# Linear attention with its first rows normed under the weight loads and its query squares on GpSimd; row attention with two groups of heads packed

## The reference

```python
def softmax_kernel_features(data, proj, is_query):          # 12 heads of 16, 44 features
    data_dash = jnp.einsum('bhnd,md->bhnm', data_normalizer * data, proj)
    diag_data = jnp.sum(jnp.square(data), axis=-1, keepdims=True) * 0.5 * data_normalizer ** 2
    stab = jnp.max(data_dash, axis=-1, keepdims=True) if is_query else jnp.max(data_dash)
    return ratio * (jnp.exp(data_dash - diag_data - stab) + EPS)
q, k, v = (x @ W_qkv)                                       # x is the layer-normed stream
q1, k1 = softmax_kernel_features(q, proj_mat, True), softmax_kernel_features(k, proj_mat, False)
kv, ksum = jnp.einsum('bhnm,bhnd->bhmd', k1, v), jnp.sum(k1, axis=2)
z = 1.0 / jnp.einsum('bhnm,bhm->bhn', q1, ksum)
out = (jnp.einsum('bhnm,bhmd->bhnd', q1, kv) * z[..., None]) @ W_proj + b_proj
...
attn = jax.nn.softmax(jnp.einsum('bhnd,bhmd->bhnm', q, k) * hd ** (-0.5), axis=-1)
o = jnp.einsum('bhnm,bhmd->bhnd', attn, v).transpose(0, 2, 1, 3).reshape(B, N, C)
return o @ proj_w + proj_b
```

## Time and profile before

| | us |
|---|---|
| three runs | 2276.53, 2280.19, 2281.41 |
| median | 2280.19 |
| profiled execution | 2284.59, span 2282.7 |
| TensorE busy in the span | 1844.9 (81%) |
| VectorE busy | 1344.2 (59%) |
| ScalarE busy | 1055.9 (46%) |
| GpSimd busy | 563.8 (25%) |
| linear attention, first block to its end | 109 to 490 |
| row attention, second block with its tail | 1632 to 1925 |

### The profile page before, as it was taken

One profiled execution on the slowest core, in us unless ns is written; L12 is line 12 of the kernel. 1 busy time (PEld: TensorE's weight loads), 2 busy tenths in 40 slices (PEclk: granted clock), 3 DMA queues, 4 the chain that ended last, 5 costly groups with the idle time before them and its releaser, 6 DMA issues. The chain is left out here.

```text
span 2282.7 us, 30822 instructions
## 1 busy us (share of the span) xinstructions
PE 1844.9 (81%) x9746; PEld 993.9 (44%) x9746; DVE 1344.2 (59%) x2464; ACT 1055.9 (46%) x1916; POOL 563.8 (25%) x708
## 2 busy tenths in 40 slices
PE   5789889958756447777489977999899993999998
PEld 4645755535324320000122244443134343888887
DVE  6446359946111779999678876999655553222211
ACT  2011322214001659999689964333387870222222
POOL 5000000000212017767200003332014443333333
PEclk9989999958887675555599978997699995999999
DMA  3010110024996005234101008788777634577774
GB/s 89 7 44 28 55 35 22 19 91 182 408 408 265 1 18 180 89 116 134 32 26 32 28 17 124 125 125 126 83 89 108 96 95 144 164 210 202 198 212 104
DMA packets 153120, 258.49 MB, mean 113 GB/s; under 512 B 28560, under 2 KB 124673, under 8 KB 148006
## 3 DMA queue, kind: packets, MB, share of 16 engines
q1 hardware_dynamic: 134822, 239.15, 39.8%
q0 software_dynamic: 18176, 17.80, 4.0%
HBM read 215.16 MB, written 57.51 MB: 119 GB/s over the span
## 5 line engine op out<-in xcount | busy, mean ns | idle before, releaser
L1734 PE MATMUL ps<-arena 128*128 x384 | 198.1, 621 | 82.8 <-ACT ps L1817 62.0
L1817 ACT ACTIVATE ps<-ps,arena 128x512 f32<-128x512 f32 x384 | 256.1, 724 | 9.1 <-POOL arena L1798 9.1
L1744 DVE TENSOR_REDUCE arena<-ps 128x1024 f32 x192 | 232.8, 1224 | 29.0 <-PE ps L1734 18.0
L2186 DVE TENSOR_REDUCE arena<-ps 128x1024 f32 x192 | 221.1, 1213 | 11.9 <-PE ps L2432 9.5
L2655 ACT ACTIVATE arena<-ps 128x1024 f32<-128x1024 f32 x192 | 185.8, 1022 | 90.6 <-PE ps L2533 89.5
L2992 ACT ACTIVATE arena<-ps,arena 128x256 f32<-128x256 f32 x234 | 89.7, 482 | 235.8 <-PE ps L2957 235.7
L2432 PE MATMUL ps<-arena 96*128 96x512 bf16 x500 | 163.6, 432 | 25.0 <-DVE arena L2186 11.5
L1976 ACT ACTIVATE arena<-ps 128x1024 f32<-128x1024 f32 x192 | 178.9, 1043 | 10.6 <-DVE arena L1996 5.2
L2927 POOL DMA_INDIRECT out_dram<-arena x78 | 121.2, 1554 | 238.6 <-DVE arena L3016 168.6
L3012 DVE TENSOR_TENSOR arena<-ps,arena 128x384 f32<-128x384 f32 x39 | 21.8, 558 | 258.7 <-PE ps L2968 258.7
L531 PE MATMUL ps<-arena 96*128 96x456 f32 (+1 forms) x512 | 168.7, 481 | 6.0 <-DMA arena<-la_xt 4.8
(11 more groups left out here) (395 smaller groups left out, 3144.9 us busy)
## 6 DMA issues: line engine op xcount, KB each, us to landing
arena<-in_sm_w_dram SPq DMA_DIRECT2D x128, 576.0 KB, 16.6
arena<-in_re_w_dram SPq DMA_DIRECT2D x39, 1252.0 KB, 5.9
arena<-ra_parts SPq DMA_DIRECT2D x192, 192.0 KB, 9.6
routed_in<-routed_in SPq DMA_DIRECT2D x8, 3332.0 KB, 14.0
ra_parts<-arena SPq DMA_DIRECT2D x48, 192.0 KB, 2.4
arena<-routed_in SPq DMA_DIRECT2D x39, 196.0 KB, 5.4
arena<-la_xt SPq DMA_DIRECT2D x16, 384.0 KB, 3.4
arena<-arena SPq DMA_DIRECT2D x64, 96.0 KB, 2.2
```

The lines of the kernel that those rows point to most:

```text
L1734: ins = pe.matmul(ps[:, 2 * (n % 4) + t % 2, :], QM[j][:, h, t * P:(t + 1) * P], KI[:, b, h // HG, :], start=True, stop=True)
L1744: v.tensor_reduce(MXq[:, b, 2 * u:2 * u + 2, at_head(h)], ps[:, 2 * (n % 4):2 * (n % 4) + 2, :], AX.X, ALU.max).then_inc(s_lk, 1)
L1817: ins = act.activation(bank, bank, ACT.Exp, bias=nb[n % 4][:, t % 2:t % 2 + 1], scale=c_reg, accum_out=RS[:, b, t, at_head(h):at_head(h) + 1])
L2186: v.tensor_reduce(MX[:, bass.ds(b, 1), 2 * (n % 2):2 * (n % 2) + 2, n // 2].rearrange("p o t -> p (o t)"), ps[:, 2 * (n % 2):2 * (n % 2) + ...
```

## The change

Three things. In the linear attention's first block the norm, the turn (into banks 4 and 5) and the copy of batch 0 now stand before the weight products and their results; the second half of the weight products (banks 4 to 7) waits for the copy; the 11 loads count on three semaphores, of which TensorE waits for `s_wt` (`WT` and `BD`), VectorE for `s_w` (`W`), and `s_wp` is awaited before the query block's products. In the query pass VectorE's product L820 is gone: GpSimd squares `SQ` in place when VectorE has copied it, and VectorE waits for it before the sum. In row attention the groups 0 and 1 are packed: `OP` takes group 0 to the first 16 of 32 columns and group 1 to the other 16, group 2 stands alone with zeros beside it, so that two transposes and a contraction over two groups are left; `OS` is one buffer; the rows of `Wp` come in 12 DMAs.

```diff
@@ -459,20 +459,38 @@
     S1 = lambda n, per=1, credit=1: Signal(nc, f"la_{n}", per, credit)
     ln_v, ln_s = layer_norm_constants(nc, m, "la_ln")
     s_zr = sem("la_fill_zeroed")
-    s_w, s_bd, s_wx, s_wxc, s_mask = (sem(f"la_{n}") for n in (
-        "weights_loaded", "zeros_set", "wx_ready", "wx_copied", "mask_set"))
+    s_wt, s_w, s_wp, s_bd, s_wx, s_wxc, s_mask = (sem(f"la_{n}") for n in (
+        "feature_weights_loaded", "weights_loaded", "projection_loaded", "zeros_set", "wx_ready", "wx_copied",
+        "mask_set"))
+    xn, xt, xc, kp, ksq, kd = S1("rows_normed"), S1("rows_turned"), S1("rows_turned_copied"), \
+        S1("k_products", T, T + 1), S1("k_squared", T), S1("k_features", T, 2)
+
+    def norm(v, b):
+        xt.wait(v, b, 0)
+        for t in range(T):
+            ins = v.tensor_scalar(XN[:, t, :], m.H[:, bass.ds(b, 1), t, :].rearrange("p o d -> p (o d)"),
+                                  m.mean[:, bass.ds(b, 1), t], m.rstd[:, bass.ds(b, 1), t], ALU.subtract, ALU.mult)
+        ins.then_inc(xn.sem, 1)
+
+    def turn(pe, b):
+        xn.wait(pe, b, 1)
+        xc.wait(pe, b, 0)
+        for c in range(NC):
+            for t in range(T):
+                ins = pe.transpose(ps[0:DC, 4 + c, t * P:(t + 1) * P], XN[:, t, c * DC:(c + 1) * DC], m.ident)
+        ins.then_inc(xt.sem, 1)
 
     with nc.Block(no_gpsimd_drain=True) as block:
         @block.sync
         def _(sp):
-            sp.dma_start(WT, io.la_WT[0:2 * D, :].rearrange("(s p) n -> p s n", s=4)).then_inc(s_w, 16)
+            sp.dma_start(WT, io.la_WT[0:2 * D, :].rearrange("(s p) n -> p s n", s=4)).then_inc(s_wt, 16)
             sp.wait_ge(s_bd, 1)
             for h in range(6):
-                sp.dma_start(BD[h * HD:(h + 1) * HD, h * NF:(h + 1) * NF], io.la_projT).then_inc(s_w, 16)
+                sp.dma_start(BD[h * HD:(h + 1) * HD, h * NF:(h + 1) * NF], io.la_projT).then_inc(s_wt, 16)
             sp.dma_start(W, io.la_W.rearrange("(c p) n -> p c n", c=NC)).then_inc(s_w, 16)
-            sp.dma_start(Wp[:, 0, :], io.la_Wproj[0:P, :]).then_inc(s_w, 16)
-            sp.dma_start(Wp[0:D - P, 1, :], io.la_Wproj[P:D, :]).then_inc(s_w, 16)
-            sp.dma_start(Wp[D - P:D - P + 1, 1, :], io.la_b[None, :]).then_inc(s_w, 16)
+            sp.dma_start(Wp[:, 0, :], io.la_Wproj[0:P, :]).then_inc(s_wp, 16)
+            sp.dma_start(Wp[0:D - P, 1, :], io.la_Wproj[P:D, :]).then_inc(s_wp, 16)
+            sp.dma_start(Wp[D - P:D - P + 1, 1, :], io.la_b[None, :]).then_inc(s_wp, 16)
             sp.wait_ge(s_bd, 2)
 
             sp.dma_start(io.routed_in[NX * PART * TR:(NX * PART + 1) * TR].rearrange("(p h) d -> p (h d)", h=2),
@@ -499,12 +517,19 @@
 
         @block.scalar
         def _(act):
+            xc.start(act)
             ln_s(act)
+            xt.wait(act, 0, 1)
+            act.activation(XTs[0], ps[0:DC, 4:6, :], ACT.Copy).then_inc(xc.sem, 1)
 
         @block.tensor
         def _(pe):
-            pe.wait_ge(s_w, 16 * 11)
+            xt.start(pe)
+            turn(pe, 0)
+            pe.wait_ge(s_wt, 16 * 7)
             for s in range(2):
+                if s == 1:
+                    xc.wait(pe, 0, 1)
                 for c in range(NC):
                     for half in range(2):
                         ins = pe.matmul(ps[0:DC, 4 * s + 2 * c + half, 0:FH],
@@ -513,8 +538,10 @@
 
         @block.vector
         def _(v):
+            xn.start(v)
             ln_v(v)
-            v.wait_ge(s_w, 16 * 11)
+            norm(v, 0)
+            v.wait_ge(s_w, 16)
             for s in range(2):
                 v.tensor_copy(Wx[:, s, :, 0:D], W[:, :, s * D:(s + 1) * D])
             v.wait_ge(s_wx, 1)
...
@@ -786,8 +789,8 @@
     QD = [g4(P, [2 * FH]) for _ in range(2)]
     KX = [g4(2 * NF, [2, 6, 2, HD]) for _ in range(2)]
     SUMS, RD, TN, OT = g4(P, [S]), g4(P, [S // 32, 2]), g4(P, [S]), g4(P, [2, S])
-    qp, qd, qe, qt, qc = S1("q_products", T, T + 1), S1("q_features", T, 2), S1("q_exp", T, 2), \
-        S1("q_turned", T, 2), S1("q_turned_copied", T, 2)
+    qp, qk, qsq, qd, qe, qt, qc = S1("q_products", T, T + 1), S1("q_copied", T), S1("q_squared", T), \
+        S1("q_features", T, 2), S1("q_exp", T, 2), S1("q_turned", T, 2), S1("q_turned_copied", T, 2)
     num, ot, pr, hh = S1("read_out", 2, 3), S1("normalised", 2), S1("projected"), S1("stream_updated")
     s_qk, s_rd = sem("la_q_chain"), sem("la_reciprocal")
     xq = [sem(f"la_q_rows{j}_loaded") for j in range(2)]
@@ -815,9 +818,9 @@
                 j = t % 2
                 qp.wait(v, b, t + 1)
                 q = ps[:, 2 * j, 0:D]
-                v.tensor_copy(SQ[j], q)
-                link(v.tensor_reduce(mq[j].rearrange("p (g h) -> p g h", g=2), features(t), AX.X, ALU.max))
-                link(v.tensor_tensor(SQ[j], SQ[j], q, ALU.mult))
+                v.tensor_copy(SQ[j], q).then_inc(qk.sem, 1)
+                v.tensor_reduce(mq[j].rearrange("p (g h) -> p g h", g=2), features(t), AX.X, ALU.max)
+                qsq.wait(v, b, t + 1)
                 squared_lengths(v, link, t)
                 link(v.scalar_tensor_tensor(out=dg[j], in0=dg[j], scalar=0.125, in1=mq[j], op0=ALU.mult,
                                             op1=ALU.add))
@@ -847,7 +850,7 @@
                                m.H[:, bass.ds(b, 1), t, :].rearrange("p o d -> p (o d)"))
 
             def batch(b, behind, last_behind):
-                link = Link(v, s_qk, b * (4 * T))
+                link = Link(v, s_qk, b * (2 * T))
                 chain(b, link, 0)
                 if last_behind:
                     add(b - 2)
@@ -867,6 +870,15 @@
             normalise(B - 1, 0)
             normalise(B - 1, 1)
             add(B - 1)
+
+        @block.gpsimd
+        def _(pool):
+            for s in (qk, qsq):
+                s.start(pool)
+            with pool.Fori(0, B) as b:
+                for t in range(T):
+                    qk.wait(pool, b, t + 1)
+                    pool.tensor_tensor(SQ[t % 2], SQ[t % 2], SQ[t % 2], ALU.mult).then_inc(qsq.sem, 1)
 
         @block.scalar
         def _(act):
@@ -942,6 +954,7 @@
                     read_out(b - 1, 1 - j, 1)
                 turn(b, 2)
 
+            pe.wait_ge(s_wp, 16 * 3)
             batch(0, 0, 0, False, False)
             batch(1, 0, 1, True, False)
             with pe.Fori(1, B // 2) as i:
@@ -2063,7 +2076,7 @@
     TMP, OQ = fx(P, [NG, S]), [fx(P, [NG, S], BF16) for _ in range(2)]
     OF, WPb, inv3, s_out, magic, weights_end = m.quantised
     MX = g2(P, [B, T, NH])
-    Wp, bp = g2(P, [NG, D]), g2(P, [D])
+    Wp, bp = g2(P, [2, D]), g2(P, [D])
     spare = g2(P, [1])
     mark = g2.at
     XN, XT = g2(P, [T, D]), [g2(DC + 1, [NC, S]) for _ in range(2)]
@@ -2349,8 +2362,9 @@
                 sp.dma_start(gb[:, 1, :], io.ra_ln1_b.rearrange("(c p) -> p c", c=NC)).then_inc(s_w, 16)
             sp.wait_ge(s_z, 1)
             for j in range(HG):
-                sp.dma_start(Wp[32 * j:32 * j + HD], io.ra_Wproj.rearrange(
-                    "(g j d) n -> j d g n", g=NG, j=HG)[j]).then_inc(s_w, 16)
+                for g in range(NG):
+                    row, head = 32 * j + HD * (g % 2), HD * (HG * g + j)
+                    sp.dma_start(Wp[row:row + HD, g // 2, :], io.ra_Wproj[head:head + HD, :]).then_inc(s_w, 16)
             with sp.Fori(0, B // 2) as i:
                 for j in range(2):
                     b = 2 * i + j
@@ -2473,7 +2487,7 @@
 
     g4 = Cut(m.arena, mark, END)
     PF = [g4(P, [HG, S]) for _ in range(2)]
-    OT, OS, per_sum = g4(P, [NG, S]), g4(P, [NG, S]), g4(P, [S // 32])
+    OT, OP, OS, per_sum = g4(P, [2, S]), g4(P, [2, S]), g4(P, [S]), g4(P, [S // 32])
     VT = V.rearrange("p b (t h n) -> p b t h n", t=T, h=NH)
     NS = NG * T
     st, ex, av = S1("scores_turned", 2 * NS, 2 * NS + 1), S1("exp", 2 * NS, 3), S1("read_out", NS, NS + 1)
@@ -2541,10 +2555,10 @@
                 elif bank > 5:
                     xx.wait(pe, b, 1)
                 for t in range(2):
-                    for g in range(NG):
+                    for k in range(2):
                         q = (2 * half + t) * P
-                        ins = pe.matmul(ps[:, bank, t * D:(t + 1) * D], OT[:, g, q:q + P], Wp[:, g, :],
-                                        start=(g == 0), stop=(g == NG - 1))
+                        ins = pe.matmul(ps[:, bank, t * D:(t + 1) * D], OT[:, k, q:q + P], Wp[:, k, :],
+                                        start=(k == 0), stop=(k == 1))
                 ins.then_inc(pr.sem, 1)
 
             def turn_rows(p, c, bank):
@@ -2671,6 +2685,7 @@
         def _(v):
             for s in (os_, ot, xx):
                 s.start(v)
+            v.memset(OP[:, 1, :], 0.0)
             v.wait_ge(s_bt, B // 2)
             v.tensor_copy(*turned_parts(B // 2 - 1, 7)).then_inc(s_bc, 1)
             chain, gate = Link(v, s_l3), Link(v, s_gl)
@@ -2776,13 +2791,15 @@
                     if b and g == 2:
                         logits(b - 1, 7 - j)
```

(10 more changed lines are left out.)

30 lines of the change are left out of this document (4 added, 26 removed).

## The result

The changed kernel takes 2250.1 us (median; 2246.97 to 2254.1), beside 2280.3 us of the kernel before on the same chip (2276.53 to 2281.41): ratio 0.9866, 95% interval 0.9848 to 0.9885. That is 30 us less where 23 were forecast: the sign was right, and the time fell on the lower edge of the range. The profiled execution took 2254.1 us (span 2252.0), so the two profiled spans differ by 30.7 us.

The account below looks back on a forecast made before the run. No single bound: TensorE paces the query pass with VectorE right behind, ScalarE is busiest in row attention, and nothing overlaps in the opening. Savings 6.5 + 5.5 + 11 = 23 us take 2280.2 to 2257.2 us, range 2250 to 2269.

Parts of the forecast that it names:

- Part A: Linear attention's opening: shorter load wait and batch 0's preparation under the loads save 6.5 us, range 5.4 to 9.
- The wait: Opening: TensorE awaits only query/key weights and projection loads, so weight products start at 115.1 instead of 117.1: 2.0 us.
- norm, turn and copy: Opening: batch 0's preparation goes under the weight loads, removing 4.43 us before the first key product.
- the clock, which I bounded: Opening: TensorE's clock over the weight products, bounded from a 1.0 us loss to a 2.5 us gain.
- Part B: Query pass: squares move from VectorE to GpSimd, removing TensorE's waits; 5.5 us, range 3 to 8.
- One bound of the prediction: Query pass: if GpSimd's product costs 1.06 us, the sum starts 0.23 us later, a loss of 3 us.
- The first rival: Query pass: GpSimd's square waits for VectorE's maximum, losing 7 us instead of winning 5.5; 2269.7 us, chance 0.09.
- the step for the last batch: Query pass: beyond 5.3 us over some seven batches, a little more where TensorE idles longer; 5.5 taken.
- Part C: Row attention: two packed groups cut projection records from 12 to 8 in 16 calls; 11 us, bounds 9 and 12.
- the third rival: Row attention: fewer projection records drop TensorE's clock; with half the stage so, 2341 us, chance 0.03.
- The second rival: Row attention: ScalarE's exponentials set the pace, so packing leaves only the tail's 1.3 us; 2266.9 us, chance 0.07.
- the signs of being wrong: Longer query-pass batch, ScalarE still idling 2 us per row-attention projection, or the clock in either stage leaving 1.00.

Follow-up runs that it names:

- e1: Kernel before with only the linear attention's opening changed (batch 0 normed, turned and copied under the weight loads, shorter wait): 2275.92 us, ratio 0.9971.
- e9: Changed kernel with TensorE again waiting for all 11 opening loads before the weight products: 2255.51 us, one execution.
- e3: Kernel before with only row attention's packing into two groups: 2272.46 us, ratio 0.9946.
- e8: Changed kernel with a second, unread GpSimd square before the one that counts, so VectorE's sum waits longer: 2264.25 us, one execution.
- e2: Kernel before with only the query pass's squares moved to GpSimd: 2268.96 us, ratio 0.994.
- e4: Changed kernel run again with no edit: 2249.68 us, ratio 0.9865.
- e7: Changed kernel with row attention's projections multiplying the first packed group twice, so calls have twelve records again: 2256.33 us, one execution.
- e11: Changed kernel with unread TensorE products only at the start of the mixture of 64 experts: 2256.52 us, ratio 0.9888.
- e5: Kernel before with unread TensorE products in its waits in the query block's last two batches: 2274.42 us, ratio 0.9959.
- e6: Changed kernel with unread TensorE products in its waits in the query block's last two batches: 2253.56 us, ratio 0.986.
- e10: Changed kernel with unread TensorE products both in the query pass's last two batches and at the mixture's start: 2253.29 us, ratio 0.9866.

## Why the prediction was right in its parts and short in its sum

**Part A, forecast 6.5 us (5.4 to 9): 7.4 and 8.3 us** in the profiles of the change and of `e1`. The wait was worth 2.2 us between the two profiles and 2.4 by `e9`, not 2.0; norm, turn and copy gave 4.1 of the 4.4 told (from the end of the weight products to the first key product 3.3 us instead of 7.4); the clock, which I bounded and put at nearly nothing, gave 1.0 us in the change and 1.9 in `e1` (5.64 and 4.71 us for 6.66, at a mean granted clock of 0.66 and 0.79 for 0.56). The clock's is the term of this part that was mis-sized. Counted from the first load's issue, the weight products started after 5.5 us (told: 5.7) and the first key product after 14.4 (told: 15.3).

**Part B, forecast 5.5 us: 5.7 in the pass, but some 14 in the kernel.** The steps for the pass held: the square took 505 ns (estimated 590), the hand-over 0.08 us (0.15), the sum started after 0.94 us (1.11), and TensorE's waits of 0.76 us a batch went. A steady batch lost 0.88 us (19.96 to 19.08), a little more than the waits, while the pass as a whole lost 5.7 us and not 7; that 5.5 was met so closely is partly luck. One bound of the prediction was added up short: a sum that starts 0.23 us later costs 0.92 us a batch, less 0.4 to spare, which over eight batches is 4 us and not 3. The first rival falls: the maximum took 697 ns at the median beside the square, 696 in the kernel before. Of the two places of the Trainium skill, the trace agrees with the lock told in "SBUF — State Buffer" ("SBUF: two separate sides"), which leaves a maximum over PSUM free. The warning in "Perfetto Trace Analysis" ("Optimizing Scalar/DVE Operations") that moving operations between VectorE and GpSimd might not help did not come true here.

The step that failed is the one for the last batch: "a little in the last batch, where TensorE idles longer", together with the boundary that I drew around the pass. I had priced the waits of a steady batch and then stopped; that TensorE's clock could change in this part, I put at nothing without a reason. The runs showed 5.2 us there, 0.9 of them waits and 4.3 the clock, and 2.2 behind. Before, TensorE waited 0.34 and 1.86 us for the last two copies and ran the projection behind them at the lower level; after, the first wait is gone, the second is 1.36 us, and the upper level lasts through the projection and the read-out behind it. What I showed for this: the stretch is 36.1 us in all four kernels whose chain is as long as before (before, `e1`, `e3`, `e8`), 30.9 in the six with the short chain and no filling (after, `e2`, `e4`, `e7`, `e9`, `e11`), and 27.4 (`e5`, long chain) and 26.6 to 26.7 (`e6`, `e10`, short chain) where TensorE was filled.

The 2.2 us before the experts go with part B: 76.0 us (75.9 to 76.1) in the five profiles with the short chain and nothing unread, 77.8 to 78.5 in the four with the long one. The difference lies in the clock of the last 20 us (0.77 before, 1.00 in the last 18 after): the same products take 3.34 us before and 2.00 after (TensorE's timelines, before, then after).

```profile
561.30 3.34 PE L1200 MATMUL ps<-arena 128*128 128x64 f32 x24
```

```profile
545.10 2.00 PE L1213 MATMUL ps<-arena 128*128 128x64 f32 x24
```

That this stretch follows the length of the chain is shown both ways, by `e2` and `e8`. That it follows from a shorter end of the query block is not: `e5`, `e6` and `e10` shorten that end further, and the stretch takes 80.4 to 80.7 us. Why the clock shifts so far behind stays open.

The 2.4 us of row attention's first part are less sure. In the change they came with a higher clock (0.80 over the stretch for 0.71), but `e2` took 63.4 us at 0.72, `e5`, with the long chain, 61.8, `e7` 59.6 and `e10`, with the short one, 65.8. Over thirteen profiles this stretch took 59.6 to 66.3 us. What sets the clock in it stays open; it can't be booked to part B or to the change.

**Part C, forecast 11 us (9 to 12): 8.6 in the change, 9.3 in `e3`.** The first lies below my own bound. The price of a call was 0.65 us instead of 0.69, the tail 1.4 instead of 1.3, the zero fill (0.48 us at 1611.19, before the first exponentials' data were there) and the eight loads cost nothing to be seen. Fourteen calls should give 9.1 (the forecast had 9.6); the stage gave 7.2. Most of the missing 1.9 us is a second dip of the clock. A dip is a pair of longer waits of ScalarE at one place of a batch, behind sixteen small products of the gate (the change, ScalarE's and TensorE's timeline):

```profile
1668.04 1.95 PE L2574 MATMUL ps<-arena 96*128 96x8 f32 x16
...
1670.80 1.87 PE L2613 MATMUL ps<-arena 128*32 128x512 f32 x8
...
1672.60 1.88 PE L2547 MATMUL ps<-arena 99*128 99x512 bf16 x4
...
1673.67 1.94 ACT L2669 ACTIVATE arena<-ps 128x1024 f32<-128x1024 f32 x2 [1.26 <-PE ps L2547]
...
1676.05 1.02 ACT L2669 ACTIVATE arena<-ps 128x1024 f32<-128x1024 f32 x1 [0.44 <-PE ps L2547]
```

At this place without a dip neither wait is there (`e4` runs its five exponentials through), so one costs 1.26 + 0.44 = 1.7 us. Counting dips by windows of 3 us sorts all thirteen profiles:

| records in a call | dips | first to last score product, us | profiles |
|---|---|---|---|
| 12 | none | 242.9 | `e5` |
| 12 | one | 244.5 to 246.0 | before, `e1`, `e2`, `e7` |
| 8 | one | 234.8, 234.9 | `e10`, `e11` |
| 8 | two | 237.0 to 238.3 | after, `e3`, `e4`, `e6`, `e8`, `e9` |

At one dip each the difference is 244.9 - 234.9 = 10.0 us, but not all of it is packing: in `e10` and `e11` ScalarE's third wait at the start of the stage is 0.7 us, against 1.75 in the other profiles but `e3` (1.62), as the clock rises 5.8 to 5.9 us after the first score product and not after 7.8 to 9.1. Without that 1 us, packing is worth some 9 us at equal dips, the 9.1 of the calls; in the change the second dip takes 1.7 of them back. This is the third rival in small: its mechanism (fewer records, lower clock) did occur, at two places instead of over half the stage. That fewer records cause the second dip isn't shown: `e10` and `e11` have eight records and one dip, and `e5` has none with twelve. The second rival falls, as ScalarE's wait fell with the records. Of the signs of being wrong that I had named, one did come: the clock in the stage left 1.00. It was a poor sign, as the kernel before has a dip too, at 1788.8 us, outside the window of 1642 to 1668 us that I had read.

**The sum.** 7.4 + 5.7 + 8.6 = 21.7 us lie where 23 were forecast; 5.2 + 2.2 us lie just behind part B and came with it; the remaining 1.6 of the spans' 30.7 us is what the stretches that none of this decides add up to (+2.5, +0.5, -2.4, -1.5, -0.7).

## What to carry to other kernels

Price a removed wait of TensorE also in the stretches behind the loop: ask at which clock the drain runs, what TensorE did just before it, and what it would take at the other level (here 5.5 us of projection for 2.9, a read-out of 3.64 us for 1.92). Give a gain of some 10 us in a stage at full clock a band of two us or so for dips (1.7 us each here), as they come and go with edits elsewhere, and compare stages at equal numbers of dips before judging an edit. Unread products can hold the clock through a drain, but look at the next stretch before believing them: in the changed kernel the 4.3 us that they won came back as a loss of 4.4, and in the kernel before 2.4 of 8.7 did.
